# Six score banks in attention's last head, two search pieces exchanged, tensors begun on 128-byte lines, and a new place for two pieces of work in the FFN's chunks

## What is computed

```python
def _L0_attn_ref(x, ...):              # x: (2, 2048, 256), 16 heads of 16
    attn = einsum('bhqd,bhkd->bhqk', q, k) / sqrt(d)
    attn = where(causal, -inf, attn) + rpb[rel_idx]
    w = softmax(attn); o = einsum('bhqk,bhkd->bhqd', w, v)
    y = x + (o @ proj_w.T + proj_b)
    return layernorm(y) * ln_g + ln_b
def _fused_branch(Q, K, V, W, U, b, router...):   # twice, 8 experts of rank 64
    prod = (Q @ V) * cumsum(K @ W)
    weights = softmax(gelu(Q @ w1 + b1) @ w2 + b2)
    return ((prod * weights) @ U + weights @ b) / n_valid
def _L1_attn_ref(u, ...):              # a state-space scan
    dt = softplus(u @ W_dt.T + b_dt + dt_bias)
    ...
x = layernorm(x + _L0_attn_ref(x)); x = layernorm(x + _L0_ffn_ref(x))
x = layernorm(x + _L1_attn_ref(x)); x = layernorm(x + _L1_ffn_ref(x))
```

## Time and profile before

| | us |
|---|---|
| median of 3 runs | 2452.58 |
| lowest and highest run | 2452.12, 2458.05 |
| the profiled execution, its own time | 2455.18 |
| its span, first to last instruction | 2453.5 |
| attention's head -1 and all before it | 0 to 114 |
| heads 0 to 14 | 114 to 928 |
| head 15 | 928 to 984 |
| FFN: folding of weights, then 8 chunks | 988 to 1036, 1036 to 1486 |
| scan and mixture of experts | 1486 to 2453.5 |

### The profile page before, as it was taken

The page is one execution under the profiler, slowest core; times in us unless marked ns, Lnnn a source line. Parts: engine busy times, 40 slices in busy tenths (PEclk is TensorE's granted clock), DMA queues, the critical chain, the costliest instruction groups (busy, mean ns, idle before and its releaser), DMA issues. The chain is left out here.

```text
span 2453.5 us, 40617 instructions
## 1 busy us (share of the span) xinstructions
PE 2320.9 (95%) x13519; PEld 1495.4 (61%) x13519; DVE 1922.3 (78%) x4360; ACT 1423.4 (58%) x2606; POOL 1043.5 (43%) x1031
## 2 busy tenths in 40 slices
PE   8999999999999999899999999999999998999992
PEld 5433333333333333577777777788888776887782
DVE  3888888888888881557666658999999989898366
ACT  3477676676666667334545546665656676654420
POOL 3512212211122111100000004999999887898364
PEclk9999999999999999999999999999999999999996
DMA  8643222223332202100000001111111232225694
GB/s 257 174 74 79 53 52 52 53 52 63 67 77 52 52 22 71 58 18 18 21 24 26 16 13 48 65 52 65 52 65 52 71 109 67 71 76 161 223 327 154
DMA packets 111910, 190.30 MB, mean 78 GB/s; under 512 B 15972, under 2 KB 74136, under 8 KB 108504
## 3 DMA queue, kind: packets, MB, share of 16 engines
q1 hardware_dynamic: 84472, 150.49, 23.1%
q10 hardware_dynamic: 21088, 20.45, 2.5%
q0 software_dynamic: 6144, 16.79, 2.1%
HBM read 104.39 MB, written 78.79 MB: 75 GB/s over the span
## 5 line engine op out<-in xcount | busy, mean ns | idle before, releaser
L628 ACT ACTIVATE ssm_in_dt<-att_s 128x512 f32<-128x512 f32 (+3 forms) x1280 | 600.3, 536 | 259.5 <-PE att_s L538 186.1
L538 PE MATMUL att_s<-att_qs,att_ks 64*128 64x512 f32 (+3 forms) x1280 | 445.3, 423 | 26.9 <-ACT ssm_in_dt L628 25.1
L525 PE MATMUL att_s<-att_ks,att_qs 64*128 64x512 f32 (+3 forms) x1280 | 442.2, 424 | 5.9 <-DVE ssm_in_u L762 3.9
L538 PEld LDWEIGHTS att_s<-att_qs,att_ks 64*128 64x128 f32 x1280 | 208.9, 184 | 368.6 <-ACT ssm_in_dt L628 324.1
L2415 POOL TENSOR_TENSOR ssm_cc<-ssm_cc,ssm_h 128x512 f32<-128x512 f32 x256 | 331.6, 1295 | 81.3 <-DVE ssm_h L2511 69.5
L2424 POOL TENSOR_TENSOR ssm_out_z<-ssm_out_z,ssm_cc 128x512 f32<-128x512 f32 x256 | 336.2, 1313 | 0.1
L449 POOL TENSOR_SCALAR_AFFINE_SELECT ssm_in_dt<-ssm_in_dt 128x256 f32<-128x256 f32 x256 | 104.1, 407 | 545.9 <-ACT ssm_in_dt L628 532.8
L571 PE MATMUL att_o_ps<-ssm_in_dt,att_vst 128*32 128x512 f32 (+3 forms) x2560 | 302.0, 544 | 2.3 <-ACT ssm_in_dt L628 0.8
L2202 ACT ACTIVATE ssm_cc<-seam_banks,seam_par 128x512 f32<-128x512 f32 x256 | 198.4, 775 | 155.6 <-PE seam_banks L1996 155.3
L727 DVE CUSTOM_DVE_ANT_0 att_hid<-att_s,att_hidden 128x512 bf16<-128x512 f32 (+3 forms) x512 | 226.1, 487 | 68.7 <-PE att_s L525 68.4
L721 DVE CUSTOM_DVE_ANT_0 att_hid<-att_s,att_near 128x512 bf16<-128x512 f32 x384 | 246.2, 686 | 30.2 <-PE att_s L525 30.0
(11 more groups left out here) (366 smaller groups left out, 4195.4 us busy)
## 6 DMA issues: line engine op xcount, KB each, us to landing
qk_halves<-ssm_in_dt SPq DMA_DIRECT2D x64, 256.0 KB, 3.1
scan_halves<-seam_block SPq DMA_DIRECT2D x32, 512.0 KB, 2.9
seam_block<-scan_halves SPq DMA_DIRECT2D x32, 512.0 KB, 3.5
moe_sorted<-att_hidden SPq DMA_DIRECT2D x31, 512.0 KB, 9.6
moe_answers<-ssm_cc ACTq DMA_DIRECT2D x62, 256.0 KB, 4.0
att_stage_q<-qk_halves SPq DMA_DIRECT2D x96, 128.0 KB, 4.4
att_stage_k<-qk_halves SPq DMA_DIRECT2D x96, 128.0 KB, 6.0
ssm_raw<-in_w_bc SPq DMA_DIRECT2D x30, 256.0 KB, 3.3
```

The source lines that it names most:

```text
L525: mm = nc.tensor.matmul(s1[:, S1_BANK[at], 0:hi - lo], qs[p % 3][half(b), I * P:(I + 1) * P], ks[p % 3][half(b), lo:hi], start=True, stop= ...
L538: mm = nc.tensor.matmul(s2[:, turn % RING, 0:hi - lo], ks[p % 3][half(b), J * P:(J + 1) * P], qs[p % 3][half(b), lo:hi], start=True, stop= ...
L628: nc.scalar.activation(prob[:, b, step % 2, x * CH + lo:(x + 1) * CH], s2[:, turn % RING, 0:CH - lo], ACT.Exp, scale=1.0 / HD).then_inc(s2 ...
```

## The change

1. `score_banks` gives the scores of head 15, from step 2 on, six banks in turn (0 to 5) in place of three; the first score in a bank of the search waits until the last transposed output of head 14 has been read. In these steps the loop of TensorE is also ordered anew: both batches' scores, then `add_far`, then, in slots 1 and 3, a half of the sums.
2. In `SEARCHED` the piece (15, 3), 512 wide, and the piece (8, 2), 128 wide, trade places: (8, 2) is now searched in step 5, slot 3, and (15, 3) in step 6, slot 0.
3. `Space.line` pads the attention's tensors so that each begins at a multiple of 128 bytes; in the FFN 96 bytes are put ahead (`begin`), and the large tensors are declared first, so that they begin on such lines too.
4. FFN: the `x1T` entries of `ORDER` move from the end of group 4 to group 5, ahead of its `weight` entries. ScalarE runs `add_bias` before `write_x1`, `read_x1` in group 5, `expn_of` in group 6, and `log_of` after both `round_hi`, at the chunk's end. VectorE runs `correction` at the chunk's end, between `running_sum` and the second `round_lo`.

```diff
-            (14, 2), (15, 2), (11, 2), (15, 3),
-            (8, 2), (12, 3), (9, 2), (13, 3),
+            (14, 2), (15, 2), (11, 2), (8, 2),
+            (15, 3), (12, 3), (9, 2), (13, 3),
...
+WIDE = NP2 * (PAIRS - 1) + 2 * SLOTS * 2
+def score_banks():
+    banks, free, used = {}, {}, {}
+    for turn in range(NP2 * PAIRS):
+        bank = RING + turn % RING if turn < WIDE else (RING + turn - WIDE + WIDE % RING) % (2 * RING)
+        banks[turn], free[turn] = bank, used.get(bank, -1) + 1
+        used[bank] = turn
+    return banks, free
+S2_BANK, S2_FREE = score_banks()
...
-                after(eng, s2_read, turn - RING + 1)
+                after(eng, s2_read, S2_FREE[turn])
                 if turn == 0:
                     eng.wait_ge(s1_read, ALONE)
+                if S2_BANK[turn] < RING and S2_FREE[turn] == 0:
+                    eng.wait_ge(s1_read, S1_AT["out", PAIRS - 2, 1] + 1)
...
                     for x in range(SLOTS):
+                        if p == PAIRS - 1 and step >= 2:
+                            for b in range(2):
+                                score(p, step, x, b)
+                            add_far(p, step, x)
+                            if x in (1, 3):
+                                sums(p, step - 1, x // 2)
+                            continue
                         for b in range(2):
...
+    def line(self, name, shape, dt=F32):
+        size = 2 if dt == BF16 else 4
+        for n in shape[1:]:
+            size *= n
+        tensor = self.sb(name, shape, dt)
+        size += -size % ROOM
+        if size % LINE:
+            self.sb(f"{name}_end", [P, (LINE - size % LINE) // 4])
+        return tensor
...
+        begin = sp.sb("begin", [P, 24])
+        res = sp.sb("res", [P, TPC, D])
+        ky = sp.sb("ky", [P, 2, CH])
...
             if g == 4:
                 ORDER += [("dt", m) for m in range(KT)]
+            if g == 5:
+                ORDER += [("x1T", k) for k in range(KT)]
             ORDER += [("weight", n) for n in WEIGHED.get(g, ())]
-            if g == 4:
-                ORDER += [("x1T", k) for k in range(KT)]
...
                     if g == 4:
                         turned(c)
-                        if not last:
-                            write_x1(c)
                         if not first:
                             add_bias(c)
                         if not last:
-                            read_x1(c, raw)
-                    if not first and g == 5:
+                            write_x1(c)
+                    if g == 5 and not last:
+                        read_x1(c, raw)
+                    if g == 6 and not first:
                         expn_of(c)
-                    if not first and g == 6:
-                        log_of(c)
                 if not last:
                     for a in range(2):
                         round_hi(c, raw, a)
+                if not first:
+                    log_of(c)
...
-                    if g == 5 and not first:
-                        correction(c)
                 if not last:
                     round_lo(c, raw, 0)
                     running_sum(c, raw)
+                if not first:
+                    correction(c)
+                if not last:
                     round_lo(c, raw, 1)
```

More of the change, by code:

```diff
@@ L29 @@
 START = 1
+ROOM, LINE = 32, 128
 ROUNDED = 2
@@ L234, in phase_attention @@
         sp = Space(nc, ctx, "att")
[L235 to L239, removed]
-        prob = Region(t.dt_sb)(2, 2, S)
[L241 to L251, removed]
+        stage = [sp.line(f"stage_{n}", [P, S]) for n in "qk"]
+        qs = [sp.line(f"qs{s}", [P, S], F32R) for s in range(3)]
+        ks = [sp.line(f"ks{s}", [P, S], F32R) for s in range(3)]
+        near = [sp.line(f"near{s}", [P, SPAN], BF16) for s in range(2)]
+        far = [sp.line(f"far{s}", [P, WIN], BF16) for s in range(2)]
+        prob = Region(t.dt_sb)(2, 2, S)
+        vst = [[sp.line(f"vst{s}{b}", [P, TB, 32]) for b in range(2)] for s in range(2)]
+        partmax = sp.line("partmax", [P, 2, TB, 4])
+        mx = [sp.line(f"mx{n}", [P, 2, HALF]) for n in range(2)]
+        mxT = [sp.line(f"mxT{n}", [2 * HALF, P], F32R) for n in range(2)]
+        oT = [sp.line(f"oT{b}", [P, CH]) for b in range(2)]
+        rsum = sp.line("rsum", [P, 4, 4])
+        ident = sp.line("ident", [P, P])
+        flip = sp.line("flip", [PARTS * QUARTER, QUARTER])
+        flip_b = sp.line("flip_b", [P, QUARTER], BF16)
+        hidden = sp.line("hidden", [P, CH])
+        hid = [sp.line(f"hid{n}", [P, CH], BF16) for n in range(4)]
         s12 = sp.psum("s12", [P, 2 * RING, CH])
-        s1, s2 = s12, s12[:, RING:2 * RING]
+        s1 = s12
         o_ps = sp.psum("o_ps", [P, 2, CH])
@@ L534, in score @@
                 turn = NP2 * p + 2 * (SLOTS * step + x) + b
-                after(eng, s2_read, turn - RING + 1)
+                after(eng, s2_read, S2_FREE[turn])
                 if turn == 0:
                     eng.wait_ge(s1_read, ALONE)
-                mm = nc.tensor.matmul(s2[:, turn % RING, 0:hi - lo], ks[p % 3][half(b), J * P:(J + 1) * P],
+                if S2_BANK[turn] < RING and S2_FREE[turn] == 0:
+                    eng.wait_ge(s1_read, S1_AT["out", PAIRS - 2, 1] + 1)
+                mm = nc.tensor.matmul(s12[:, S2_BANK[turn], 0:hi - lo], ks[p % 3][half(b), J * P:(J + 1) * P],
                                       qs[p % 3][half(b), lo:hi], start=True, stop=not has_far)
@@ L551, in add_far @@
                         at = far_lo - (J + FAR) * P + P - (g + 1) * QUARTER
-                        mm = nc.tensor.matmul(s2[quarter(g), (turn + b) % RING, far_lo - lo:hi - lo], flip_b[:], far[p % 2][:, at:at + hi - far_lo],
+                        mm = nc.tensor.matmul(s12[quarter(g), S2_BANK[turn + b], far_lo - lo:hi - lo], flip_b[:], far[p % 2][:, at:at + hi - far_lo],
                                               start=False, stop=True)
@@ L627, in exponential @@
                 eng.wait_ge(s2_ready, turn + 1)
-                nc.scalar.activation(prob[:, b, step % 2, x * CH + lo:(x + 1) * CH], s2[:, turn % RING, 0:CH - lo],
+                nc.scalar.activation(prob[:, b, step % 2, x * CH + lo:(x + 1) * CH], s12[:, S2_BANK[turn], 0:CH - lo],
                                      ACT.Exp, scale=1.0 / HD).then_inc(s2_read, 1)
@@ L834, in phase_fused @@
         sp = Space(nc, ctx, "ffn")
+        begin = sp.sb("begin", [P, 24])
+        res = sp.sb("res", [P, TPC, D])
+        ky = sp.sb("ky", [P, 2, CH])
+        wp = sp.sb("wp", [P, KT, D])
+        pb, gain, bump = sp.sb("pb", [P, D]), sp.sb("gain", [P, D]), sp.sb("bump", [P, D])
+        x = sp.sb("x", [P, TPC, D])
+        y = sp.sb("y", [P, TPC, D])
+        x1 = sp.sb("x1", [P, TPC, D])
+        oT = sp.sb("oT", [P, 2, KT, P])
         ident, idb = sp.sb("ident", [P, P]), sp.sb("idb", [P, P], BF16)
+        wT = sp.sb("wT", [NSP * NW, CH], BF16)
+        wst = sp.sb("wst", [P, TPC, NSP, NW], BF16)
         router = sp.sb("router", [P, KT, 2 * NW])
@@ L847, in phase_fused @@
         hi, lo = t.row_hi, t.row_lo
-        res = sp.sb("res", [P, TPC, D])
-        ky = sp.sb("ky", [P, 2, CH])
         lgT = raw[:, 1, 1]
@@ L857, in phase_fused @@
         wrest = sp.sb("wrest", [P, TPC, NW])
-        wst = sp.sb("wst", [P, TPC, NSP, NW], BF16)
-        wT = sp.sb("wT", [NSP * NW, CH], BF16)
         stats = sp.sb("stats", [P, TPC, 6])
@@ L864, in phase_fused @@
         x_hi, x_lo = (room[:].rearrange("p a k c -> p a (k c)") for room in t.block)
-        wp = sp.sb("wp", [P, KT, D])
-        pb, gain, bump = sp.sb("pb", [P, D]), sp.sb("gain", [P, D]), sp.sb("bump", [P, D])
         keep = sp.sb("keep", [P, NCH])
[L868 to L871, removed]
         stats1 = sp.sb("stats1", [P, TPC, 6])
```

## The result

The changed kernel takes 2431.05 us (median of 4 runs, 2429.42 to 2432.64); the kernel before, measured beside it, 2453.23. The ratio is 0.9903, with a 95% interval of 0.9889 to 0.9917: 1% faster, some 22 us. The profiled execution took 2432.64 us, its span is 2430.9.

The account below looks back on a forecast made before the run. Bounds taken: TensorE and VectorE in heads 0 to 14, TensorE in FFN chunks, TensorE-ScalarE coupling in head 15. Gains 8.0 + 2.5 + 0 + 6.0 = 16.5 us took 2452.6 to 2436.1, 8-in-10 range 2427 to 2445.5.

Parts of the forecast that it names:

- Head 15: From step 2 on, six banks cut ScalarE's idle time from 10.8 to 3.5 us; gain 8.0, bounds 4 and 12.
- The merging of bursts: In head 15, bursts of exponentials that merge gain up to 2 us more (sixteen bursts, some 0.12 each).
- The clock: Two slow-clock stretches, in head 15's step 6 and at the last sums: no gain counted, 3.4 us as a bound.
- The exchanged pieces: Search banks awaited less at step 5's end: 0.17 us a head, 2.5 in 15 heads, bounds -1.5 and 6.0.
- Lines: Tensors beginning on 128-byte lines in attention and FFN: priced at nothing, bounds -1 and +1 us.
- Chunks 1 to 6: FFN gaps ahead of `x1T` (0.84) and last `w` (0.79) go, a 0.45 wait comes: 1.18 us each, 7.1 together.
- Chunk 0: FFN's first chunk loses only the gap ahead of `x1T`: 1.42 us less 0.4, so 1.0 gained.
- The seam: FFN's end to the scan: the later logarithm delays VectorE's tail, the barrier awaits it; 2.1 us lost.
- sums couple: Rival in head 15: the sums, not the banks, couple TensorE and ScalarE; gain 1 for 8, 2443.1 us, chance 0.12.
- the FFN pays back: Rival: `minus_abs` still meets GpSimd, new wait 1.0, tail 3.5; FFN gains 0.6 for 6.0, 2441.5 us, chance 0.13.
- the exchange costs: Rival in step 6 of every head: wide pieces cost 15 x 1.1 = 16.5 us, total 2455.1, chance 0.04.
- more half clock in head 15: Rival: four slow stretches in head 15 in place of two cost 3.4 us more, 2439.5 us, chance 0.07.

## Why the prediction was right, and where its terms were off

Forecast 2436.1 in a range of 2427.0 to 2445.5; measured 2431.05. The direction and the mechanisms held. The forecast gain was 16.5 us, the measured one 22. By the table of stretches nearly all terms erred the same way: heads 0 to 14 gave 2.1 us more than forecast, the chunks 1 to 6 2.1, chunk 0 1.4, the last sums 1.4, the end of the FFN 0.5, head 15 0.3 less; the stretches that are not the change's took back 1.2.

1. **Head 15: 8.0 forecast, 7.7 measured, but made up differently.** "10.8 idle, 3.5 stay" became 10.8 to 4.0: 1.9 at step 6 (2.0 forecast), 1.0 at step 8 (1.0), 1.1 in steps 2 to 5 (0.5). The merging of bursts, allowed "up to 2", gave 1.4 (28.7 to 27.3), as a part of the same sum. Of the 7.7 some 1.4 are the clock's: taking for each step the least time of the four traces with three banks and the old order gives 49.7 for a head 15 at full clock, so the banks and the order are worth 6.3.
2. **The clock: "I count none" was wrong.** Both stretches of the earlier trace rows are gone, 1.4 us in step 6 and 1.4 at the last sums, 2.8 of the 3.4 bound. With three banks and the old order all four traces have such a stretch in head 15, worth 1.4, 2.7, 4.5 and 4.5 us against 49.7; with six banks one of nine has (1.6). So the kernel before was exposed to up to 4.5 us, of which its own profile showed 1.4. The rule of the Trainium skill ("TensorE: Matmul & The Clock Gate", "A second HAM failure mode: psum-queue depth-cycling"), read as "more cycling through banks, more slow stretches", did not hold here: more banks went with fewer. But the section names short idles of TensorE together with the cycling, and the change alters where these stand as well: from the stretch's rows, TensorE idles 3.3 of 31.3 us now. Three banks in the new order had no slow stretch in the one trace there is, with TensorE idle for 4.4 of 39.3 us, so neither the number of banks nor the sum of the idles is shown to be the cause; it stays open.
3. **The exchanged pieces: 2.5 forecast, 4.2 to 4.6 measured** (15 times 0.28 to 0.30). The term that was mis-sized is "0.17 us a head": it counted the end of step 5 alone. Both steps fell by 0.13. VectorE's idle time in step 6, one wait of 0.98 in the earlier trace rows, is 0.80 now in two, and the pieces around it start closer together: from the second wide piece of step 5 to the end of the last narrow one it was 4.60 us (472.38 to 476.98) and is 4.33 (473.07 to 477.40).

```profile
474.29 0.28 DVE L763 CUSTOM_DVE_ANT_0 att_hid<-att_s,att_hidden 128x128 bf16<-128x128 f32 x1
...
474.85 0.29 DVE L763 CUSTOM_DVE_ANT_0 att_hid<-att_s,att_hidden 128x128 bf16<-128x128 f32 x1 [0.27 <-PE att_s L552]
...
477.11 0.29 DVE L763 CUSTOM_DVE_ANT_0 att_hid<-att_s,att_hidden 128x128 bf16<-128x128 f32 x1 [0.53 <-PE att_s L552]
```

4. **Lines: nothing forecast, nothing measured.**
5. **Chunks 1 to 6: 1.18 forecast, 1.54 measured each.** All three places were right, the price of a gap too low. "Gap plus 0.16" leaves out the restart: behind a wait the matmul takes 0.50 us and the next starts 0.34 after it, where in the stream starts are 0.23 apart. By starts, `x1T`'s gap was worth 1.20 (forecast 0.84), the last `w`'s 0.93 (0.79), the new one cost 0.48 (0.45); these make 1.65, of which a chunk shows 1.54. `minus_abs` was short in every trace with `x1T` late, as forecast, so the price put on a long one (a new wait of 1.0) was not tried.
6. **Chunk 0: 1.0 forecast, 2.4 measured.** At the end of the idle 1.26 of the earlier trace rows a half-clock stretch began, which the prediction had in its bounds but not in its sum. All five traces in which `x1T` comes early have this idle and four have the stretch; of the nine in which it comes late, none has it. It is worth 1.4 us (`x1T` early: chunk 0 at 56.6 to 56.9 with the stretch, 55.26 in the one trace without).
7. **The seam: 2.1 lost forecast, 1.5 measured;** chunk 7's own loss 0.2 forecast, 0.1 measured. VectorE's tail began 8.35 us ahead of TensorE's last output's end (7.9 forecast) and took 9.9 us (10.1). The mechanism is shown by the run that puts it back.

Of the rivals none came about: three refuted by runs (sums couple; the FFN pays back; the exchange costs), the fourth, more half clock in head 15, by nine traces.

## What to carry to other kernels

When two engines wait for each other by turns and both have slack, count how far ahead the producer may run before changing any order: here the order paid only once the banks were there. Before moving a piece of work, list what it covers at its old place; `dt` covered the copy of `wT`, and moving it cost more than the wait it was to fill. Price a removed gap of TensorE by the distance of starts around it, not by the idle time that is shown, and look for a half-clock stretch behind it (here behind idles of 1.26 us in four of five cases and of 2.2 us in three of six).

## What the hardware showed that was not expected

- Half clock (granted 0.5, the 1.2 GHz level) does not come in every execution at the same place. Its stretches last 3.4 to 17 us in these traces, apart from one of 42 to 46 us that every trace has at its very end. Kernels alike up to the first exponential reach it between 116.4 and 119.2 us. One trace can miss a cost of 1 to 4 us that the next one has.
- The three sets ran the kernel before in 2454.7, 2489.15 and 2485.02 us. The changed kernel, traced twice, agrees within 2 us up to 2220 us; the 31.6 us by which the spans differ stand behind that, in the mixture of experts, where the DMA engines move 240 GB/s in one trace and 208 in the other. First the trace after, then its repeat:

```profile
2220.00:2431.00 211.00, 162.69 (x957) 133.56 (x957) 117.72 (x325) 63.81 (x112) 113.00 (x117) 0.90 0.74 240
```

```profile
2220.00:2462.50 242.50, 172.80 (x950) 138.47 (x948) 116.17 (x322) 63.00 (x111) 111.91 (x115) 0.87 0.66 208
```

The other traces agree: between 2225 and 2400 us the DMA engines move 248 to 264 GB/s in the four of the first set and 220 to 233 in the eight of the other two. That stage, not the ones changed here, makes the difference between the three chips; why was not tried.
